# Attention scores in three rounded products: both parts made by GpSimd, neighbours swapped by DMA, four exponentials ahead of the output's copy

## The reference

```python
q = apply_rope(split_heads(x @ Wq)); k = apply_rope(split_heads(x @ Wk)); v = split_heads(x @ Wv)
sim = jnp.einsum('bid,bjd->bij', q, k) * scale        # causal mask, then softmax
out = jnp.einsum('bij,bjd->bid', softmax(sim), v)
x = _layernorm(x + out @ Wo + bo)
...                                                    # top-2 of 8 experts, gelu, weighted sum
# apply_rope: rot = stack([x1 * cos - x2 * sin, x1 * sin + x2 * cos]) with x1, x2 = even, odd channels
```

## Time and profile before

| | |
|---|---|
| median of 3 runs | 832.34 us (831.88 to 833.89) |
| profiled execution | 833.57 us, its span 831.8 us |
| PE busy | 808.2 us, 97% |
| DVE busy | 676.2 us, 81% |
| ACT busy | 623.1 us, 75% |
| POOL busy | 554.5 us, 67% |
| DMA, mean over the span | 55 GB/s |

### The profile page before, as it was taken

The page is one execution under the profiler, slowest core; times in us unless marked ns, Lnnn a source line. Parts: engine busy times, 40 slices in busy tenths (PEclk is TensorE's granted clock), DMA queues, the critical chain, the costliest instruction groups (busy, mean ns, idle before and its releaser), DMA issues.

```text
span 831.8 us, 21102 instructions
## 1 busy us (share of the span) xinstructions
PE 808.2 (97%) x6267; PEld 591.3 (71%) x6267; DVE 676.2 (81%) x2711; ACT 623.1 (75%) x1672; POOL 554.5 (67%) x612
## 2 busy tenths in 40 slices
PE   8999999999999999999999999999999889999995
PEld 4566666666666666666666666666666569999995
DVE  6887798889888988898889988988898856225996
ACT  4677787888788878887887778777877766555576
POOL 5765646456756775667568866775687236899893
PEclk9999999999999999999999999999999999999999
DMA  5111101000100010001001100100012246424435
GB/s 164 33 40 40 52 20 33 8 20 27 52 14 27 27 39 15 29 27 36 17 27 31 36 18 23 41 25 15 14 47 83 61 130 205 132 82 127 129 113 156
DMA packets 55438, 46.09 MB, mean 55 GB/s; under 512 B 6368, under 2 KB 47072, under 8 KB 55328
## 3 DMA queue, kind: packets, MB, share of 16 engines
q1 hardware_dynamic: 50960, 35.90, 15.1%
q0 software_dynamic: 4224, 8.72, 3.1%
q10 hardware_dynamic: 144, 0.13, 0.1%
HBM read 28.39 MB, written 12.14 MB: 49 GB/s over the span
## 4 chain that ended last, share of the span: by engine, by line
PE 92%; DVE 3%; issue 2%; ACT 1%; DMA 1%; POOL 0%; another core or an unknown queue 0%; SPq 0%; DVEq 0%; ACTq 0%
PE TB L1026 18%; PE S_all L979 18%; PE TB L1010 14%; PE S_all L1177 7%; PE AO L1047 7%; PE TB L1190 4%; PE AO L1190 4%; PE S_all L1010 3%; PE AO L908 3%; PE AO L906 3%; PE AO L907 3%; PE AO L970 1%; PE AO L968 1%; PE AO L969 1%; PE AO L903 1%
## 5 line engine op out<-in xcount | busy, mean ns | idle before, releaser
L1295 ACT ACTIVATE Pr_all<-Sm,nmax 128x512 f32<-128x512 f32 (+3 forms) x512 | 280.6, 554 | 0.0
L1504 DVE CUSTOM_DVE_ANT_0 Sm<-S_all,causal 128x512 f32<-128x512 f32 (+3 forms) x512 | 220.1, 486 | 66.6 <-PE S_all L979 66.5
L665 POOL TENSOR_TENSOR shared<-shared,sin_t 128x512 f32<-128x512 f32 x63 | 80.3, 1275 | 168.5 <-DVE shared L1484 168.3
L1307 ACT ACTIVATE PT<-TB 128x1024 f32<-128x1024 f32 x185 | 131.0, 742 | 63.8 <-PE TB L1010 63.5
L979 PE MATMUL S_all<-kT,qT 64*128 64x512 f32 (+3 forms) x1024 | 166.7, 443 | 1.9 <-POOL kT L668 0.9
L1026 PE MATMUL TB<-PT,shared 128*64 128x128 f32 x1008 | 151.2, 441 | 5.3 <-ACT PT L1307 0.3
L1525 DVE SCALAR_TENSOR_TENSOR x_acc<-AO,rinv,x_acc 128x128 f32<-128x128 f32 x504 | 141.7, 344 | 4.1 <-remote 1.9
L1010 PEld LDWEIGHTS TB<-ident,Pr_all 128*128 128x128 f32 x1000 | 108.0, 141 | 38.3 <-ACT Pr_all L1295 21.1
L1010 PE MATMUL TB<-ident,Pr_all 128*128 128x128 f32 x1000 | 133.7, 277 | 0.5 <-ACT PT L1307 0.5
L979 PEld LDWEIGHTS S_all<-kT,qT 64*128 64x128 f32 x1024 | 78.9, 187 | 71.2 <-issue 54.4
L1026 PEld LDWEIGHTS TB<-PT,shared 128*64 128x64 f32 x1008 | 69.9, 137 | 58.3 <-issue 39.4
(11 more groups left out here) (320 smaller groups left out, 1418.4 us busy)
## 6 DMA issues: line engine op xcount, KB each, us to landing
wo<-in_wo SPq DMA_DIRECT2D x64, 64.0 KB, 1.8
PT<-yrows SPq DMA_DIRECT2D x7, 512.0 KB
w_tile<-in_wup SPq DMA_DIRECT2D x10, 256.0 KB
xt<-xrows SPq DMA_DIRECT2D x32, 65.0 KB
x_acc<-in_x SPq DMA_DIRECT2D x8, 256.0 KB
wdown<-in_wdown SPq DMA_DIRECT2D x8, 256.0 KB, 3.2
pay<-pay SPq DMA_DIRECT2D x8, 256.0 KB
x_acc<-pay SPq DMA_DIRECT2D x8, 256.0 KB
```

The lines of the kernel that those rows point to most:

```text
L665: nc.gpsimd.tensor_tensor(k_rot, k_rot, sin_t[:, :], ALU.mult).then_inc(k_mul, 1)
L1295: nc.scalar.activation(Pr[j][:, 0:n], Sm[j], ACT.Exp, bias=nmax[:, j:j + 1], scale=-1.0, accum_out=rsum[p][:, h * QB + qb:h * QB + qb + 1] ...
L1307: last = nc.scalar.activation(PT[p][:, :, 0:qb + 1, qb * P:qb * P + P], source, ACT.Copy)
L1504: nc.vector.tensor_tensor_reduce(out=Sm[j], in0=SB[2 * (group % 2) + h][:, at:at + n], in1=causal[:, T - n:T], scale=-0.125, scalar=HUGE, ...
```

## The change

Scores of blocks 1 to 3, from unit 2 on (`PLAIN = 2`), are three products of rounded parts, as the projections already are; block 0 (128 columns) and the first two units stay float32. GpSimd makes the four parts `k_hi, q_hi, k_lo, q_lo` of each unit. To do the rotation, VectorE now multiplies the projection by cos and by sin, both from PSUM; the swap of neighbours is made by two DMAs for k and two for q on SyncE's queue, each of 64 rows of 512 elements (128 KB), straight into `kT[p]` and `qT[p]`; GpSimd then only adds in place. In units 0 and 1 VectorE swaps with a shuffle instead. On ScalarE `exp(u, 0)` moves ahead of `copy_v`, and `exp(u, 2)` and `exp(u, 3)` come ahead of `copy_o`, into the end of unit u. In group 1 block 0 now comes before block 2. The buffers are packed anew (`PT_all`, `Pr_all` without the unused columns; the parts share memory with what is used only after the attention).

```diff
+AHEAD_EXPS = 4
+PLAIN = 2
+SWAPPED = 2 * 16
...
 @block.sync, at the end of unit u:
+                if u + 2 < UNITS:
+                    swap_k(u + 2, p)
+                    swap_q(u + 2, p)
+            def swap_k(u, p):
+                sp.wait_ge(k_read, u + 1)
+                wait(sp, scored, BLK * (u - 1))
+                sp.dma_start(kT[p][0:P:2, :], k_rot[1:P:2, :]).then_inc(k_swapped, 16)
+                sp.dma_start(kT[p][1:P:2, :], k_rot[0:P:2, :]).then_inc(k_swapped, 16)
...
 @block.gpsimd
             def rotate_k(u, p):
-                pool.wait_ge(k_read, u + 1)
-                nc.gpsimd.tensor_tensor(k_rot, k_rot, sin_t[:, :], ALU.mult).then_inc(k_mul, 1)
-                wait(pool, scored, BLK * (u - 1))
-                pool.wait_ge(k_mul, u + 1)
-                nc.gpsimd.tensor_tensor(kT[p][:, :], k_cos, k_rot, ALU.add).then_inc(k_ready, 1)
+                pool.wait_ge(k_swapped, SWAPPED * (u + 1))
+                nc.gpsimd.tensor_tensor(kT[p][:, :], k_cos, kT[p][:, :], ALU.add).then_inc(k_ready, 1)
+            def high_q(u, p):
+                pool.wait_ge(q_ready, u + 1)
+                nc.gpsimd.tensor_copy(q_hi[p][:, :], qT[p][:, P:T]).then_inc(qk_high, 1)
+            def split_q(u, p):
+                pool.wait_ge(qk_high, 2 * (u - PLAIN) + 2)
+                nc.gpsimd.tensor_tensor(q_lo[p][:, :], qT[p][:, P:T], q_hi[p][:, :], ALU.subtract).then_inc(qk_split, 1)
...
                     rotate_k(u + 2, p)
                     rotate_q(u + 2, p)
+                    high_k(u + 2, p)
+                    high_q(u + 2, p)
+                    split_k(u + 2, p)
+                    split_q(u + 2, p)
...
 @block.tensor, score:
+                    for h in range(2):
+                        nc.tensor.matmul(banks[h], q_hi[p][halves[h], rows], k_hi[p][halves[h], 0:n], start=True, stop=False)
+                    for h in range(2):
+                        nc.tensor.matmul(banks[h], q_hi[p][halves[h], rows], k_lo[p][halves[h], 0:n], start=False, stop=False)
+                    for h in range(2):
+                        nc.tensor.matmul(banks[h], q_lo[p][halves[h], rows], k_hi[p][halves[h], 0:n],
+                                         start=False, stop=True).then_inc(scored, 1)
...
+                else:
+                    pe.wait_ge(qk_split, 2 * (u - PLAIN) + 2)
...
 @block.scalar, attention:
-                    for j in range(2, BLK):
+                    for j in range(AHEAD_EXPS, BLK):
                         exp(u - 1, 1 - p, j)
...
                     copy_pt(u - 1, 1 - p, 0)
+                exp(u, p, 0)
                 if 1 <= u <= VBLOCKS - QB:
                     copy_v(QB + u - 1)
...
-                exp(u, p, 0)
-                exp(u, p, 1)
+                for j in range(1, AHEAD_EXPS):
+                    exp(u, p, j)
...
 @block.vector, rope_q (rope_k alike):
                 nc.vector.tensor_tensor(q_cos, bank[:, :], cos_t[:, :], ALU.mult)
-                nc.vector.stream_shuffle(q_rot, bank[:, :], swap).then_inc(q_read, 1)
+                nc.vector.tensor_tensor(q_rot, bank[:, :], sin_t[:, :], ALU.mult).then_inc(q_read, 1)
+                if u < PLAIN:
+                    dve.wait_ge(q_read, u + 1)
+                    nc.vector.stream_shuffle(qT[u % 2][:, :], q_rot, swap).then_inc(q_swapped, SWAPPED)
```

More of the change, by code:

```diff
@@ L3 @@
 from contextlib import ExitStack
+from itertools import accumulate
 F32 = mybir.dt.float32
@@ L143, in sb, with in_turn @@
             return ctx.enter_context(nc.sbuf_tensor(name, shape, dtype))
+        def in_turn(first, then):
+            with ExitStack() as attention_only:
+                held = [attention_only.enter_context(nc.sbuf_tensor(*of)) for of in first]
+            return held, sb(*then)
         def ps(name, shape=(P, 512)):
@@ L190, in build_block @@
         Sm = [Sm_of[qb][:, h, :] for h, qb in ORDER]
-        Pr_all = sb("Pr_all", [P, BLK, T])
-        Pr = [Pr_all[:, i, :] for i in range(BLK)]
+        (Pr_all, *q_parts), f_acc = in_turn(
+            [("Pr_all", [P, 2 * PR_BLOCKS * P], F32)] + [(f"q_part{i}", [P, T - P], F32R) for i in range(4)],
+            ("f_acc", [P, NT, C], F32))
+        q_hi, q_lo = q_parts[0:2], q_parts[2:4]
+        ends = list(accumulate((qb + 1) * P for h, qb in ORDER))
+        Pr = [Pr_all[:, end - (qb + 1) * P:end] for end, (h, qb) in zip(ends, ORDER)]
         nmax = sb("nmax", [P, BLK])
@@ L327, in build_block @@
         q_read, k_read = sem("q_read"), sem("k_read")
-        q_mul, k_mul = sem("q_mul"), sem("k_mul")
+        q_swapped, k_swapped = sem("q_swapped"), sem("k_swapped")
         q_ready, k_ready, v_ready = sem("q_ready"), sem("k_ready"), sem("v_ready")
+        qk_high, qk_split = sem("qk_high"), sem("qk_split")
         scored = sem("scored")
@@ L973, in score @@
             def score(u, p, group):
-                for i, qb in enumerate(GROUPS[group]):
-                    at = 3 * P * i
-                    for h in range(2):
-                        half = slice(D * h, D * h + D)
-                        nc.tensor.matmul(SB[2 * (group % 2) + h][:, at:at + (qb + 1) * P], qT[p][half, qb * P:qb * P + P],
-                                         kT[p][half, 0:(qb + 1) * P], start=True, stop=True).then_inc(scored, 1)
+                for qb in sorted(GROUPS[group]):
+                    at, n = 3 * P * GROUPS[group].index(qb), (qb + 1) * P
+                    banks = [SB[2 * (group % 2) + h][:, at:at + n] for h in range(2)]
+                    halves = [slice(D * h, D * h + D) for h in range(2)]
+                    if qb == 0 or u < PLAIN:
+                        for h in range(2):
+                            nc.tensor.matmul(banks[h], qT[p][halves[h], qb * P:qb * P + P], kT[p][halves[h], 0:n],
+                                             start=True, stop=True).then_inc(scored, 1)
+                        continue
+                    rows = slice(qb * P - P, qb * P)
+                    for h in range(2):
+                        nc.tensor.matmul(banks[h], q_hi[p][halves[h], rows], k_hi[p][halves[h], 0:n], start=True, stop=False)
[4 more added lines that the diff above has]
+                                         start=False, stop=True).then_inc(scored, 1)
             def transpose(u, p, group):
@@ L1483, in rope_k @@
                 nc.vector.tensor_tensor(k_cos, bank[:, :], cos_t[:, :], ALU.mult)
-                nc.vector.stream_shuffle(k_rot, bank[:, :], swap).then_inc(k_read, 1)
+                nc.vector.tensor_tensor(k_rot, bank[:, :], sin_t[:, :], ALU.mult).then_inc(k_read, 1)
+                if u < PLAIN:
+                    dve.wait_ge(k_read, u + 1)
+                    nc.vector.stream_shuffle(kT[u % 2][:, :], k_rot, swap).then_inc(k_swapped, SWAPPED)
             def first_k():
```

66 lines of the change are left out of this document (39 added, 27 removed).

## The result

The changed kernel takes 853.15 us (median of 4 runs, 849.7 to 858.7), the kernel before took 833.12 us beside it: a ratio of 1.0253, 95% interval 1.0227 to 1.0279. It is 20 us slower, where 12 us faster were forecast. The profiled execution took 850.75 us, its span is 848.8 us.

The account below looks back on a forecast made before the run. TensorE, busy 97% of the span, was taken as the bound. Terms -17.7 - 0.5 + 2 + 3 + 0.7 = -12.5 us against the 832.34 us median gave 820 us; the forecast's own range was 812 to 827, the full range 809 to 832.

Parts of the forecast that it names:

- VectorE. ... Cost 0: VectorE's product by sin replaces a 0.74 us shuffle: at most 0.1 us a unit, caught up in later units, cost 0.
- the swap at the end: At u = 60 SyncE holds the swap back behind two loads that wait for `pv_done`: 0.7 us.
- the swap is late in ordinary units: Rival: wait ahead of group 0 if the swap lands over 4.2 us after issue; at 5.3, 867 us; chance 0.08.
- TensorE: Scores fall from 2.36 to 2.02 us a unit; 0.30 taken as gain, 17.7 us over units 2 to 60.
- Loads exposed: Rival: each of the nine score pairs shows its weight load, +0.66 us a unit, 877 us; chance 0.04.
- halves in turn: Rival: rounded score products of the two heads run one after the other, +1.3 us a unit, 915 us; chance 0.05.
- streaming price: Rival: rounded score products cost streaming only, queues harmless, 0.45 us a unit gained, 809 us; chance 0.10.
- The swap: DMA swap: 0.8 us issue and 2.0 landing; k swapped at 11.4 us, q at 12.9, hidden by 2.2 us of slack.
- GpSimd overload: Around units 42 to 44 GpSimd's fuller queue makes the parts late for units 44 and 45: 3 us, ends 0 and 6.
- The start: In units 0 and 1 VectorE has three more 0.61 us steps and TensorE waits for it: 2 us, ends 0 and 3.
- ScalarE: Exponentials only move, and waits of 0.35 and 0.30 us hide the one ahead of `copy_v`: cost 0, at worst 0.1 a unit.

Follow-up runs that it names:

- version 1: The changed kernel with GpSimd making the parts for units 2 and 3 alone, later units reusing them: 820.2 us, ratio 0.9868.
- version 7: version 1 with eight GpSimd memsets of 128x384 in each unit where the parts were made: 823.65 us, ratio 0.9922.
- 4: The changed kernel with VectorE's routing operations moved behind the rotary products of their unit: 828.49 us, ratio 0.9954.
- 8: The kernel before, shuffle kept and no parts, with VectorE's routing operations behind the rotary products: 850.5 us, ratio 1.0248.
- 3: The kernel before with the DMA swap, VectorE's product by sin and GpSimd's single addition; float32 scores, no parts: 831.96 us, ratio 0.9999.
- version 2: The changed kernel with float32 scores, the parts still made and waited for but not used: 859.36 us, ratio 1.0315.
- version 12: The kernel before with ScalarE's new order alone, one exponential ahead of `copy_v` and four ahead of the output's copy: 830.23 us, ratio 1.0001.
- version 10: The changed kernel with routing behind the rotary products and the root's nine operations moved to the end of a batch's second unit: 876.32 us, ratio 1.0572.

## Why the prediction was wrong

**The step that failed** is "VectorE. ... Cost 0". It counted what VectorE's own edit adds (a product for a shuffle, 0.1 us) and left out what GpSimd's longer and later work does to VectorE's other instructions. Its price is read from the starts of group 0: from unit 6 to 62 the units of the changed kernel are together 30.8 us longer than those of version 1, 13.4 of it in the fourth units of the batches (their `project_out` waits for the rotary products that stand behind the root's operations in the third), 4.9 in the sixth, 3.8 in the fifth, 3.4 in the eighth, 3.3 in the third and 2.0 in the rest. Not all of it is this step: 2.1 us in unit 61 are the swap at the end, and 4.1 us are what GpSimd's load costs around unit 44 in version 7 (both below). That leaves some 24.6 us for the step that failed, an estimate from these rows. Seen from TensorE, the 30.8 are 20.4 us of waits for the rotary product, 2.4 of waits for the parts, 3.3 of slower work in units 35 and 44, whose granted clock is 0.88 (busy 11.89 and 12.34 us, where other fourth and fifth units have some 10.34 and 10.62), and some 5 spread over the units.

Three runs tie it down. With the same GpSimd time spent on writing alone (7), 28 us are gone. With VectorE's routing operations taken out of GpSimd's way (4), 25 are. And with them put in its way in the kernel before (8), 20 appear. That the parts themselves come late is not tested by 7, where TensorE does not wait for them; the 2.8 us that it stands still for them in the changed kernel bound it. That the swap is late in ordinary units is ruled out by 3.

The trace of before had a hint: the subtraction from `lg` has a largest time of 795 ns against a median of 192. I read means and timelines of ordinary units and did not ask of the largest. The Trainium skill ("SBUF — State Buffer", Who interferes with whom) says that a VectorE instruction with two SBUF inputs contends with a GpSimd instruction that reads SBUF, not with one that only writes, that copies and scalar operations can run in a two-port mode in which they contend with GpSimd, that reductions never do, and that the one that comes second is blocked for the whole instruction. The traces agree: up to 1217 ns beside the parts and 165 beside memsets for the two-input product, up to 441 beside memsets for the scalar operation on four columns, 186 for the reduction on `lg`, at its median and its largest. It is the rule that spoke against this change, and I had passed over it.

**TensorE.** Group 0 was forecast at 0.80 and measured at 0.82, groups 1 and 2 at 1.22 and 1.24. The gain per unit is not 0.30, though, but 0.22: ordinary units went from 10.19 to 9.97 in version 1. By the medians of units 8 to 59 its three groups gain 0.33 us, but `project_out`, up to the first product of group 1, takes 0.97 instead of 0.89, and the rest of the unit 6.98 instead of 6.94. The forecast had left both at their old length. The larger of the two is not mainly a switch from rounded to float32 work: version 2, with float32 scores in the new order, has 0.94 there. 59 x 0.22 is 13, not 17.7.

**Loads exposed, halves in turn, streaming price**: none came. Behind the first pair of a group, pairs start 0.23 to 0.25 apart at 512 columns, 0.17 to 0.18 at 384 and 0.12 at 256.

**The swap.** k's two transfers were issued from 215.02 to 216.16 us, and GpSimd's addition started at 217.75, some 1.6 us later (2.0 forecast; the issue took 1.1, not 0.8). The forecast's own terms give 11.6 for k (8.8 + 0.8 + 2.0), not 11.4, and the two copies that it took as a measure moved 512 KB against 256 for a swap, so twice as much and not four times; neither slip moves its sum by more than 0.2 us. From that addition to the end of the last subtraction are 5.7 us (forecast 6.1). No unit waits regularly for the parts; by the chain of waits TensorE's weight loads wait for `q_part` 11 times in 62 units, 11.9 us in all, and never over 2.9 us. The one place where the swap cost time is the end: SyncE issued k's swap for unit 62 only at 657.60, when VectorE's product had been ready since 655.06, and unit 61 takes 12.06 us where version 1 has 9.95, so 2.1 us where 0.7 were forecast.

**GpSimd overload**, forecast at 3 us: version 7, with the load and few held operations, has units 43 to 45 longer than version 1 by 4.1 us in all. TensorE waits there 1.5 us for rows that GpSimd normalises and 2.2 for rotary products, and not for the scores' operands as the forecast had it. **The start**, forecast at 2: unit 2 starts 1.2 us later than before. **ScalarE**, forecast at 0: shown by version 12.

The forecast's terms at these sizes give -13 - 0.5 + 1.2 + 4.1 + 2.1 = -6.1 us, some 826. Version 7, which has all of them but the last, is at 0.9922, 6.5 us under the kernel before; the terms give 8.2. So one term of some 24.6 us was missing, which makes 851 of the 826, and the gain was taken some 5 us too large.

## What to carry to other kernels

Work given to an idle engine is not free when its instructions hold up those of a busy one. Before GpSimd gets more work, list VectorE's instructions by operands: those with two SBUF inputs, and copies or scalar operations, were held here beside a GpSimd instruction that reads SBUF, and should be kept away from one. A chain of tiny dependent ones is the worst, since each link can wait for a GpSimd instruction (five of nine in version 10). Where both must stay, order VectorE so that these run in a pause that GpSimd has anyway (here, while its input is on the way by DMA), and look at largest durations, not only means.

## What the runs showed of the hardware

- A held instruction can wait for several GpSimd instructions in a row: the scalar operation on 128x16 at 470.14 took 2.60 us instead of 0.235, from a rounding across two subtractions without a gap, and ended at 472.74, just after the last (472.71) (timelines of DVE and POOL, changed kernel):

```profile
470.14 2.60 DVE L1767 TENSOR_SCALAR past<-starts_ab,tile_col 128x16 f32<-128x16 f32 x1
```

```profile
470.03 0.50 POOL L713 CAST q_part<-qT 128x384 fp32r<-128x384 f32 x1
470.50 1.26 POOL L718 TENSOR_TENSOR k_part<-kT,k_part 128x512 fp32r<-128x512 f32 x1
471.72 0.99 POOL L723 TENSOR_TENSOR q_part<-qT,q_part 128x384 fp32r<-128x384 f32 x1
```

- An operation of VectorE with one operand in PSUM was not held: in the changed kernel the score maximum over 128x384 (scores from PSUM, mask from SBUF) took 551 ns at the median in the 103 cases that fell wholly beside GpSimd's additions, roundings and subtractions, 550 in the 7 beside none, and 556 at most.
- In version 10 TensorE stood still for 5.70 us up to 120.41, and the granted clock of that unit is 0.82, a mean of the two levels of 2.4 and 1.2 GHz: 1.00 up to 118 us, 0.80 from 118 to 120, 0.50 from 120 to 126 and 0.99 from 126 to 128. The stop costs more than its length: TensorE's own busy time rose from 9.84 to 12.64 us. In the changed kernel the clock stayed at 1.00 behind waits of 1.87 and 1.92 us (units 19 and 43) and the unit's mean fell to 0.88 with waits of 1.92 and 2.12 (units 35 and 44).
